# A graph layer on one core: the last 20 chunks of each quad by indirect gathers instead of the last 12

## The reference

```python
def gnn(x, edge_index, W_lin, b_lin, W_msg, b_msg, W_upd, b_upd):
    row, col = (edge_index[0], edge_index[1])        # src, dst
    h_self = x @ W_lin + b_lin
    messages = x[col] @ W_msg + b_msg
    msg_sum = jax.ops.segment_sum(messages, row, num_segments=n_nodes)
    counts = jax.ops.segment_sum(jnp.ones((row.shape[0],), dtype=x.dtype), row, num_segments=n_nodes)
    h_agg = msg_sum / jnp.maximum(counts, 1.0)[:, None]
    h = jnp.concatenate([h_self, h_agg], axis=1) @ W_upd + b_upd
    return jax.nn.relu(h)
x = _layernorm(x + gnn(x, jnp.stack([src, dst]), ...), axis=-1)
```

## Time and profile before

| | us |
|---|---|
| median of 3 runs | 1679.45 (1676.09 to 1680.61) |
| profiled execution | 1674.59 |
| its span, first to last instruction | 1672.8 |
| TensorE busy | 1353.5 (81%) |
| VectorE busy | 1141.7 (68%) |
| ScalarE busy | 782.5 (47%) |
| GpSimd busy | 482.8 (29%) |
| mean granted TensorE clock | 0.881 of 2.4 GHz |

### The profile page before, as it was taken

How to read it: one execution, slowest core, us unless ns; L and a number is a source line. 1 busy time by engine, 2 the same in 40 slices (tenths; PEclk the granted TensorE clock), 3 DMA queues, 4 the chain that set the end, 5 groups by cost and what they waited for, 6 DMA issues and landing times.

```text
span 1672.8 us, 42910 instructions
## 1 busy us (share of the span) xinstructions
PE 1353.5 (81%) x16656; PEld 829.3 (50%) x16656; DVE 1141.7 (68%) x2880; ACT 782.5 (47%) x1128; POOL 482.8 (29%) x512
## 2 busy tenths in 40 slices
PE   3877767577675288999999999999999999999997
PEld 2767767577665134444444444444444444444443
DVE  7999999999998335555555555555555555555554
ACT  1222322100100156666666666666666666666664
POOL 1000000000000444444444444444444444444430
PEclk9777867655656589999999999999999999999998
DMA  5222122141000543343343333443444444333320
GB/s 88 83 83 102 68 83 92 55 118 43 5 1 4 181 131 106 108 113 107 116 113 114 111 112 116 116 118 117 118 117 118 116 117 119 116 116 118 117 50 11
DMA packets 119790, 160.60 MB, mean 96 GB/s; under 512 B 32099, under 2 KB 91552, under 8 KB 119516
## 3 DMA queue, kind: packets, MB, share of 16 engines
q1 hardware_dynamic: 95426, 110.08, 20.5%
q0 software_dynamic: 22880, 47.02, 12.2%
q10 hardware_dynamic: 1290, 0.78, 0.2%
HBM read 134.62 MB, written 23.21 MB: 94 GB/s over the span
## 4 chain that ended last, share of the span: by engine, by line
PE 44%; DVE 44%; issue 6%; ACT 4%; DMA 1%; DVEq 0%; SPq 0%; ACTq 0%
PE slot L1224 25%; PE acc L1238 12%; DVE big L777 5%; DVE big L757 5%; ACT big L539 4%; DVE big L919 3%; DVE big L782 3%; DVE big L788 3%; DVE big L815 2%; PE slot L1274 2%; DVE big L808 2%; PE acc L1249 2%; DVE big L968 2%; DVE big L784 2%; DVE big L929 1%
## 5 line engine op out<-in xcount | busy, mean ns | idle before, releaser
L539 ACT ACTIVATE big<-slot 128x768 bf16<-128x768 f32 x850 | 649.1, 810 | 421.4 <-PE slot L1224 382.9
L1224 PE MATMUL slot<-big 128*128 128x384 bf16 x2900 | 552.5, 328 | 90.5 <-DVE big L919 50.1
L1224 PEld LDWEIGHTS slot<-big 128*128 128x128 bf16 x2900 | 244.0, 98 | 377.9 <-DVE big L919 134.3
L625 POOL DMA_INDIRECT big<-x,dst_at x300 | 297.6, 992 | 300.3 <-PE acc L1238 172.6
L1238 PE MATMUL acc<-big 32*128 32x385 bf16 x6800 | 352.9, 325 | 0.4 <-issue 0.4
L919 DVE TENSOR_SCALAR big<-big,iota_k 128x512 bf16<-128x512 f16 x725 | 230.7, 352 | 140.8 <-PE slot L1224 128.1
L629 POOL DMA_INDIRECT big<-x,sp_i x175 | 179.0, 1023 | 280.6 <-PE acc L1257 133.0
L929 DVE TENSOR_TENSOR big<-col_lo,iota_lo 128x512 bf16<-128x512 f16 x425 | 177.8, 418 | 103.1 <-PE acc L1238 88.5
L1238 PEld LDWEIGHTS acc<-big 32*128 32x128 bf16 x6800 | 141.2, 93 | 176.4 <-issue 102.0
L1134 PE MATMUL acc<-big 125*100 125x64 f16 x1600 | 131.5, 259 | 113.7 <-DVE big L815 113.6
L1134 PEld LDWEIGHTS acc<-big 125*100 125x100 f16 x1600 | 126.2, 184 | 121.5 <-DVE big L815 121.5
(11 more groups left out here) (151 smaller groups left out, 1142.8 us busy)
## 6 DMA issues: line engine op xcount, KB each, us to landing
big<-rows SPq DMA_DIRECT2D x25, 2176.0 KB
x<-big SPq DMA_DIRECT2D x19, 480.0 KB, 2.8
big<-x SPq DMA_DIRECT2D x32, 192.0 KB, 2.5
big<-in_x SPq DMA_DIRECT2D x24, 256.0 KB
big<-base SPq DMA_DIRECT2D x24, 256.0 KB
out<-big SPq DMA_DIRECT2D x24, 256.0 KB
big<-in_x SPq DMA_DIRECT2D x19, 320.0 KB, 3.5
base<-big SPq DMA_DIRECT2D x19, 320.0 KB, 2.2
```

What stands on the lines that cost most here:

```text
L539: act.activation(xg[n % NX][:, :, 0:F3], slot[z % 2][:, :, 0:F3], ACT.Copy).then_inc(s["xg_ready"], 1)
L625: pool.indirect_dma_start(out=xg_d[:, c, 0:F3], out_offset=None, in_=x3_dram, in_offset=bass.IndirectOffsetOnAxis(ap=dst_at[:, q, c:c + 1] ...
L1224: ins = nc.tensor.matmul(slot[z % 2][:, j, 0:F3], W[R_ % NW_][:, k, (c % 4) * P:(c % 4 + 1) * P], xwin[:, win_at(c) + k, :], start=k == 0, ...
```

## The change

CP becomes 60: chunks 60 to 79, the 20 with three windows, are all fetched by indirect DMA, and the products are left for chunks 0 to 59. A quad has 15 runs with 92 products (before: 17 with 116), 10 gathered pairs (6) and the same seven spills. The gathered pairs stand in runs 3 to 12, one in each, the spills in runs 5 to 11. GATHERS has 27 entries for a quad (19), and GAP is 30 / 27. The loads of the last eight windows and the wait for them go. W gets a fourth buffer and loses its third window; `xg_d` grows to 20 chunks. The node tests of gathered pairs (`hot_dma_nodes`) are made in steps 1, 3, 5, 7 and 9 (before: 1, 5, 9).

```diff
-    CP = 68
+    CP = 60
     CD = C - CP
     NWIN = win_at(CP - 1) + n_win(CP - 1)
-    NWIN_A = win_at(60)
...
-        AREA_BYTES = 104 * 1024
+        AREA_BYTES = 116 * 1024
...
-        pre = Area(0, NWIN_A * F3 * 2)
+        pre = Area(0, WIN_BYTES)
...
-        one_a = Area(NWIN_A * F3 * 2, WIN_BYTES + AREA_BYTES)
+        one_a = Area(WIN_BYTES, WIN_BYTES + AREA_BYTES)
...
-        NB, NW_, NL, NX, ND = 2, 3, 4, 6, CD // 2
+        NB, NW_, NL, NX, ND = 2, 4, 4, 6, CD // 2
         brow = [two.take(CP * P, f16) for _ in range(NB)]
-        W = [shaped(two.take(3 * 4 * P, bf16), "p (k n) -> p k n", k=3) for _ in range(NW_)]
+        W = [shaped(two.take(2 * 4 * P, bf16), "p (k n) -> p k n", k=2) for _ in range(NW_)]
...
         RUNS = CP // 4
-        ORDER = [7, 0, 8, 1, 15, 2, 9, 3, 10, 4, 11, 5, 16, 6, 12, 13, 14]
+        ORDER = [7, 0, 8, 1, 9, 2, 10, 3, 11, 4, 12, 5, 13, 6, 14]
...
         def dma_pair_of(r):
-            return (r - 3) // 2 if r % 2 and 3 <= r < 3 + 2 * ND else None
+            return r - 3 if 3 <= r < 3 + ND else None
 
         def spill_of(r):
-            return r // 2 - 1 if r % 2 == 0 and 2 <= r < 2 + 2 * LEV else None
+            return r - 5 if 5 <= r < 5 + LEV else None
...
-                with sp.Fori(0, CP - 60) as c:
-                    load_window(bass.ds(c + 60, 1), xwin[:, bass.ds(c * 3 + NWIN_A, 3), :], 3, s["tail_wins_loaded"])
...
-                            if r % 4 == 1 and r < 2 * ND:
-                                hot_dma_nodes(q, r // 4)
+                            if r % 2 == 1 and r < ND:
+                                hot_dma_nodes(q, r // 2)
...
                     pe.wait_ge(s["W_ready"], R_ + 1)
-                    if n == 2 * ORDER.index(15):
-                        pe.wait_ge(s["tail_wins_loaded"], 16 * (CP - 60))
                     slot_free(z)
```

More of the change, by code:

```diff
@@ L229, in gnn_program @@
                  "x_turned xT_taken base_made base_taken constant_added hi_cast r1_made mid_cast lo_made OH_ready R_made R_taken Q_made route_ready T_made T_taken decoded lo_ready lo_laid lo_taken dm_ready sv_made spills_ready "
-                 "rows_stored wins_loaded tail_wins_loaded numbers_ready W_ready L_ready Ld_ready Lsp_ready gathered xg_ready ones_set "
+                 "rows_stored wins_loaded numbers_ready W_ready L_ready Ld_ready Lsp_ready gathered xg_ready ones_set "
                  "aggregated dma_added spilled sums_taken S_ready S_turned SX_taken h_made h_read y_ready var_ready std_ready normed "
```

## The result

| | median, us | runs |
|---|---|---|
| before | 1680.03 | 1676.09 to 1680.99, 4 |
| after | 1889.74 | 1889.45 to 1890.36, 4 |
| ratio | 1.1254 | 95% interval 1.1234 to 1.1273 |

The changed kernel is 210 us slower, where 115 us less was forecast. The time is outside the range of 1535 to 1615.

The account below looks back on a forecast made before the run. TensorE was taken as the bound: 1674.6 us profiled, less 98 for 24 later quads and 16 for the first, gives 1560.6, made 1565 because the runs' median is 0.3% higher. Range 1535 to 1615 us.

Parts of the forecast that it names:

- TensorE's sum: Each later quad: products and adding up saved, less gathered pairs and a spill, 5.64 - 1.36 - 0.17 = 4.1 us.
- the first quad's 16: First quad: 15 us less without the eight window loads, and a start 1 us sooner; bounds 8 to 20.
- without small waits: Case for later quads: if the small mid-quad waits go, a quad gains 5.2 us in place of 4.1.
- The cover of VectorE and ScalarE: Later quads: ScalarE falls to 24.5 of 38.9 us, VectorE loses a few of 24.58; both stay covered by TensorE.
- the small waits: TensorE's waits in mid-quad, 1.1 us in all, mechanism unknown; taken as unchanged; gain 5.2 if gone, 3.0 if doubled.
- rival 1: Small waits spread: five heavy runs a quad each start 0.78 us late, quad 41.9, time 1641 us; chance 0.19.
- GpSimd is nearly full, but not the bound: GpSimd's queue: 27 gathers a quad at 1.0 + 0.30 us make 35.1 us, under the quad's 38.9.
- Rival 3: GpSimd's gather queue becomes the bound: at 1.72 us a gather, quad 46.4, time 1747 us, slower; chance 0.04.
- the crawl: First quad, around 580 to 588 us: TensorE slow while DMA engines are full; 3.5 us, half of it, kept.
- the start came 1 us sooner: Before the first quad: the first row table, a tenth smaller, lands 1 us sooner.
- The DMA engines: Later quads: traffic rises to about 142 GB/s, under half of the full 327 GB/s; nothing taken.

Follow-up runs that it names:

- B: Condition of a whole session, cause unknown, in which the unchanged kernel before took 1640.7 to 1641.8 us; the untouched changed kernel took 1526.00 us there.
- A: Condition of a whole session, cause unknown, in which the unchanged kernel before took 1678.0 to 1680.4 us; the changed kernel's 1889.74 us was measured there.
- run 2: Not a follow-up kernel: one of the 15 numbered runs of products and adding up within a quad of the changed kernel; no time of its own is given.

## Why the prediction was wrong

**TensorE's sum was right.** The prices of the pieces gave 4.1 us a quad, if every other wait stays, and with the first quad's 16 a gain of 114 us. In B the gain is 115.8 us. In B and with plain transfers in A the quad is 37.4 us. With an even pace on both sides, in B, 68 chunks take 41.66 us a quad (620.7 to 1620.6 in 24) and 60 take 37.57 (616.1 to 1517.7): a step of 4.1. The part "without small waits", 5.2 off 42.97 for 37.8 us, comes within 0.4 of what was measured.

**The cover of VectorE and ScalarE was right.** Both have a third of the quad free, and the waits that remain are those named: VectorE before run 3, ScalarE before run 2, the transposes.

**The step that failed is the small waits.** The prediction had found them (0.43 us at 1250.42, 0.50 at 1260.81, a copy 1.38 us after its products), had noted that GpSimd issues gathers back to back beside them, wrote that the mechanism was unknown, and let them stay at 1.1 us a quad, since light and heavy runs alternate as before. They were most likely the trace of the stall. The evidence is the kernel before in B, evenly paced, where TensorE's waits from 560 us on (L1236 are its products, L1277 its transposes) are:

```profile
PE slot L1236 <- DVE big L931: 62.9, 48, 12.1
PE slot L1277 <- ACT big L539: 13.8, 24, 0.6
PE slot L1236 <- issue: 6.8, 1, 6.8
...
PE slot L1236 <- ACT big L539: 1.9, 3, 1.0
```

The 32.9 us for ScalarE before the products of the earlier trace rows are 1.9 here. The quad's 42.85 - 41.66 = 1.2 us are the 1.1 of small waits; 24 of them (28.6), 6.5 us of the first quad (57.0 and 50.5) and a start 2.6 us earlier are the 37.7 us between the two profiled runs, 1674.6 and 1636.86. Pace and condition change together here, but the pace can be only a small part: beside this run the unpaced kernel took 1640.74 in B. The term should have been priced by its cause: with 19 gathers it was 1.2 us a quad, with 27, in longer rows, 13.66 us (51.06 - 37.40). I had set it at 1.1 and bounded it by 0 and 2.2; rival 1 put it at 4.1. Rival 1, the small waits spread, named the place and the sign, but priced one wait of 0.78 us for each heavy run, where waits of 2 to 4 us and a clock at its lower level follow.

**"GpSimd is nearly full, but not the bound" was true and beside the point.** No gather was late, and nearly all that stood in a row came every 1.25 us. What was asked was only who waits for GpSimd's results. What was not asked is what GpSimd's work does to others while it runs. Rival 3, the only one that forecast a slower kernel, is refuted too, though slower it became: its gathers of 1.72 us, gap included, didn't come. The Trainium skill (SBUF — State Buffer, section "SBUF: two separate sides"), on which it leaned, describes a fight of GpSimd with VectorE; here the mean gather in A is 0.97 us, lower than before, while TensorE stands.

**The first quad was half right.** I put the crawl between 580 and 588 down to the full DMA engines. In B, with even pace, the kernel before still stands 6.8 us ("issue", the third line above, until 586.78) before the first run with three windows, where the code has TensorE wait for the eight windows, and the DMA engines are full until 584 and 96% busy on to 586.78. The first quad is 50.5 us there (570.20 to 620.74). In the changed kernel in B it is 36.8 at its own pace and 40.7 at the even one (575.46 to 616.12), a gain of 13.8 or 9.9 where 15 was forecast; the kernel before at its own pace was not traced in B. Whether the start came 1 us sooner can't be told: the first product is at 574.93 (A) and 574.23 (B), but in two traces of the kernel before it is at 572.78 and 575.61. The single matmuls, such as that at 585.45, have the other cause: they stay in A when the DMA engines are at 35%, and are gone in B.

**The DMA engines were rightly priced at nothing.** The Trainium skill (SBUF — State Buffer, section "Who interferes with whom") says that a DMA never contends with a compute engine. As far as bytes and packets go, the plain transfers bear that out, with 144 GB/s and no stall. But taken as "gathers from GpSimd are free for TensorE" it would be wrong by 364 us in condition A.

In sum, the forecast of 1565 us lies between the two times of the changed kernel, 1526.00 and 1889.74, and holds for neither. What holds is the difference in B: 115.8 us less, where 114 was forecast, since the stall that the starting time of 1679.45 contained is gone from both kernels there (the changed one has 24 x 1.5 + 5 us less than the sum's pieces). In A the small waits are twelve times as long. Which of the two the prediction would meet could not be known from the one trace that it was made from; that the small waits might grow could, and it gave that too little room.

## What to carry to other kernels

A small wait that the profile shows without a mechanism is not a constant: before a change multiplies what stands beside it (here gathers in a row, 19 to 27 a quad), find out in one experiment what it scales with. Ask of each added operation not only who waits for its result, but also whether TensorE's and the other engines' unnamed idle time ("issue", "remote") lies beside it. Where indices are known ahead or can be turned into plain ranges, try plain transfers: they were not held up in A (1520.61 us). Where gathers must be, keeping them apart in time may take off part of the stall (1727.21 us against 1889.74), and a kernel that gathers should be timed more than once, on more than one chip, before either verdict is trusted: the same pair of kernels was 12.5% slower and 7.0% faster.

## What the runs showed of the hardware

- Indirect gathers issued in a row by GpSimd can slow an engine that takes no part: in the first quad TensorE executed 22 matmuls in 20 us, one each 0.7, 1.4 or 2.1 us, where it executed 281 in the other condition. VectorE and ScalarE stood up to 7.4 and 9.3 us in the loop for signals whose sender is not named, while GpSimd's own instructions in a row kept 0.95 us and gaps of 0.30. In the first quad the stall ended 3.7 to 4.3 us after the row's last gather, in three traces.
- The effect came with the indirect form and hardly depended on the bytes: 768 or 256 bytes a row, 1889.74 or 1871.52 us; plain transfers of the same size, count and queue, of rows that lie together, 1520.61.
- It comes and goes with a condition that stayed for each of eight sessions and shows in the kernel before as 1680 or 1641 us. In its steady quads waits of 0.4 to 0.5 us were all that could be seen of it.
- Idle time is paid twice: after gaps of 0.66 and 0.60 us the granted clock was at its lower level of 0.50 from about 1240.8, stayed there over an idle time of 2.89 us, and the eight update matmuls behind it took 2.07 us in place of 1.16.
